# The expert's tile and the third output tile of layer 2 as seven block products, from the fourth batch on

## The reference

```
IN, HID, OUT, PART, E = (512, 2048, 512, 128, 8)
h = gelu(einsum('bni,ih->bnh', x, W1) + b1)          # x: 16 x 512 x 512
shared_x = einsum('bnh,ho->bno', h, W2) + b2         # W2: 2048 x 384
expert_x = einsum('bnh,bhp->bnp', h, We[indices]) + be[indices][:, None, :]
x = x + concatenate([shared_x, expert_x], axis=-1)
```

## Time and profile before

| | us |
|---|---|
| median of 3 runs | 1239.47 (1239.27 to 1239.71) |
| the profiled execution | 1239.46 |
| its span | 1237.6 |
| TensorE busy | 1233.2 |
| VectorE busy | 938.7 |
| ScalarE busy | 741.9 |

### The profile page before, as it was taken

One profiled execution on the slowest core, in us unless ns is written; L12 is line 12 of the kernel. 1 busy time (PEld: TensorE's weight loads), 2 busy tenths in 40 slices (PEclk: granted clock), 3 DMA queues, 4 the chain that ended last, 5 costly groups with the idle time before them and its releaser, 6 DMA issues.

```text
span 1237.6 us, 23847 instructions
## 1 busy us (share of the span) xinstructions
PE 1233.2 (100%) x9370; PEld 917.7 (74%) x9370; DVE 938.7 (76%) x1201; ACT 741.9 (60%) x944; POOL 0.2 (0%) x4
## 2 busy tenths in 40 slices
PE   9999999999999999999999999999999999999999
PEld 4456667777787777877877777778778777777775
DVE  6996677877777877768777688787787777877765
ACT  3756556666566665666566566565666656666553
POOL 0000000000000000000000000000000000000000
PEclk9999999999999999999999999999999999999999
DMA  7223123012030110202003020030300203011000
GB/s 274 100 72 125 43 77 95 1 35 69 0 102 0 55 47 0 102 0 68 33 0 102 0 98 4 0 101 0 102 0 21 80 0 102 0 50 52 1 35 35
DMA packets 25378, 64.45 MB, mean 52 GB/s; under 512 B 5120, under 2 KB 5376, under 8 KB 22144
## 3 DMA queue, kind: packets, MB, share of 16 engines
q1 hardware_dynamic: 25344, 63.99, 15.0%
HBM read 47.20 MB, written 16.78 MB: 52 GB/s over the span
## 4 chain that ended last, share of the span: by engine, by line
PE 98%; DVE 1%; issue 0%; ACT 0%; DVEq 0%
PE banks L1133 15%; PE banks L1134 15%; PE banks L1135 15%; PE out_ps L1135 9%; PE out_ps L1134 9%; PE out_ps L1133 9%; PE q_ps L1133 8%; PE q_ps L1134 8%; PE q_ps L1135 8%; DVE w_max L677 1%; PE out_ps L1346 1%; DVE x_lo L691 0%; PE banks L1145 0%; DVE w_lo L691 0%; PE q_ps L1145 0%
## 5 line engine op out<-in xcount | busy, mean ns | idle before, releaser
L1135 PE MATMUL banks<-x_hi,w_lo 128*128 128x256 f16 (+1 forms) x1704 | 467.0, 274 | 0.0
L1133 PE MATMUL banks<-x_hi,w_hi 128*128 128x256 f16 (+1 forms) x1704 | 467.0, 274 | 0.0
L1134 PE MATMUL banks<-x_lo,w_hi 128*128 128x256 f16 (+1 forms) x1704 | 467.0, 274 | 0.0
L691 DVE SCALAR_TENSOR_TENSOR h_ring<-u,scale,h_ring 128x2048 f16<-128x2048 f32 x120 | 281.1, 2343 | 6.9 <-ACT h_ring L456 4.8
L523 ACT ACTIVATE kept<-banks 128x512 f32<-128x512 f32 x180 | 106.3, 590 | 168.4 <-PE banks L1135 168.4
L1133 PEld LDWEIGHTS banks<-x_hi,w_hi 128*128 128x128 f16 x1704 | 166.7, 98 | 44.6 <-ACT kept L523 0.5
L1134 PEld LDWEIGHTS banks<-x_lo,w_hi 128*128 128x128 f16 x1704 | 166.7, 98 | 43.3 <-issue 0.3
L1135 PEld LDWEIGHTS banks<-x_hi,w_lo 128*128 128x128 f16 x1704 | 166.7, 98 | 21.8
L464 ACT ACTIVATE h_ring<-u,scale 128x2048 f16<-128x2048 f32 x56 | 112.1, 2002 | 90.7 <-DVE u L867 90.7
L554 ACT ACTIVATE u<-u,b_sb,undo 128x512 f32<-128x512 f32 x120 | 91.2, 807 | 124.1 <-DVE u L912 124.1
L899 DVE TENSOR_TENSOR u<-banks,kept 128x512 f32<-128x512 f32 x60 | 41.5, 692 | 154.4 <-PE banks L1135 144.8
(11 more groups left out here) (142 smaller groups left out, 1722.2 us busy)
## 6 DMA issues: line engine op xcount, KB each, us to landing
e_raw<-we_dram SPq DMA_DIRECT2D x16, 1024.0 KB, 4.7
out_dram<-x_raw SPq DMA_DIRECT2D x63, 256.0 KB, 2.3
x_raw<-x_dram SPq DMA_DIRECT2D x60, 256.0 KB, 3.6
h_ring<-w_dram SPq DMA_DIRECT2D x5, 1024.0 KB, 7.3
t_sum<-w2p_dram SPq DMA_DIRECT2D x2, 1024.0 KB, 4.8
w_sums<-w_dram SPq DMA_DIRECT2D x2, 768.0 KB, 14.6
x_raw<-x_dram SPq DMA_DIRECT2D x2, 512.0 KB, 5.8
h_ring<-w1f_dram SPq DMA_DIRECT2D x2, 512.0 KB, 7.2
```

The source lines that it names most:

```text
L691: return nc.vector.scalar_tensor_tensor(to, of, s, hi, ALU.mult, ALU.subtract)
L1133: nc.tensor.matmul(ps, hi, v_hi, start=start, stop=False, skip_group_check=True)
L1134: nc.tensor.matmul(ps, hi, v_lo, start=False, stop=False, skip_group_check=True)
L1135: return nc.tensor.matmul(ps, lo, v_hi, start=False, stop=stop, skip_group_check=True)
```

## The change

From batch 3 on (`FULL = 3`, "full" batches) output tiles 2 and 3 are a second pair that is taken in seven block products too (`mixed_unit`), so that layer 2 has 14 units of 6 narrow matmuls for a quarter. The pair mixes W2 and the expert's weights, so the sums of weight blocks are new for every batch: VectorE forms them (`add_es`, two halves a batch) from a second copy of W2's third tile, which SP loads again for each half together with the expert's half (`load_half`, twice two transfers of 512 KB, into `t_sum`), and both engines split them (`eh_split`, `es_split`). Four of the pair's products (P4, P5, P7, P6) share one PSUM bank by turns of two quarters; in between ScalarE copies it (`xy_keep`) and VectorE adds it (`take_xy`). The first two of the order in odd quarters are P4 and P5.

One scale serves all experts. It needs the largest magnitude of all eight: `all_e_tops_of` reads each expert's whole weights, which GpSimd loads one after another into one buffer of 1 MB, each after the reading of the one before. `e_top` and the scale for each batch are gone in full batches. `h_split` leaves out one of four blocks. 26 instead of 36 warm-up matmuls stand ahead of the first load.

```diff
-WARM = 36
+FULL = 3
+WARM = 26
+EVEN = ((0, P1, 0), (0, P2, 0), (1, P1, 0), (1, P2, 0), (0, P6, 0), (0, P5, 0), (0, P7, 0), (0, P4, 0),
+        (1, P4, 0), (1, P5, 0), (1, P3, 0), (0, P3, 0))
+ODD = ((1, P4, 0), (1, P5, 0), (0, P1, 0), (0, P2, 0), (1, P7, 1), (1, P6, 1), (1, P7, 0), (1, P6, 0),
+       (0, P6, 0), (0, P5, 0), (1, P1, 0), (1, P2, 0), (0, P7, 0), (0, P4, 0), (1, P3, 0), (0, P3, 0))
+FULL_UNITS = ((1, 2, 2, 2, 3, 1, 1), (2, 2, 2, 2, 3, 2, 3))
...
+            def load_half(b, half, par=None):
+                e = sp.value_load(idx[0:1, bass.ds(b, 1)], min_val=0, max_val=E - 1)
...
+                if half == 0:
+                    sp.wait_ge(x_lo_done, OPS * (b - 1) + P4 + 1)
+                else:
+                    sp.wait_ge(es_lo_done, 2 * half_number(b, half))
...
+            pool.wait_ge(w2_lo_done, D)
+            for e in range(E):
+                if e > 0:
+                    pool.wait_ge(all_e_max_done, e)
+                nc.gpsimd.dma_start(place(0, 1), we[e]).then_inc(all_e_loaded, 16)
...
+            def all_e_tops_of(*experts):
+                for e in experts:
+                    dve.wait_ge(all_e_loaded, 16 * e + 16)
+                    top(all_e_max[:, e:e + 1], place(0, 1)).then_inc(all_e_max_done, 1)
...
+            def add_es(b, half):
+                n = half_number(b, half)
+                a11, a12, a21, a22 = (eh_raw[:, :, k] for k in range(4))
+                dve.wait_ge(eh_loaded, 32 * n + 32)
+                nc.vector.tensor_tensor(a22, a21, a22, ALU.add).then_inc(es_added, 1)
...
+            def full_batch(b, par, loads=None):
+                sure = full(b - 1)
+                for i in (P4,) if first_full(b) else (P5, P7, P4):
+                    x_split(b, par, i)
+                c11(b, 0)
+                h_split(b - 1, 3, 1 - par)
+                x_split(b, par, P3)
+                add_ht(b - 1, 3)
+                eh_split(b, 0)
+                if not first_full(b):
+                    add_es(b, 0)
+                c22(b, 0)
+                ht_split(b - 1, 3, 1 - par)
...
+            def full_unit(b, d, unit):
+                units = ODD if d % 2 else EVEN
+                pair, i, back = units[unit]
+                if unit == (2 if d % 2 else 0):
+                    pe.wait_ge(h_lo_done, D * b + d + 1)
+                if unit == (0 if d % 2 else 4):
+                    pe.wait_ge(ht_lo_done, D * (b - PLAIN) + d + 1)
...
-            for unit in range(sum(Q_UNITS)):
+            for unit in range(len(EVEN)):
                 layer2(B - 1, D - 2, unit)
-
-            for unit in (0, 1, 6, 7, 8, 9, 2, 3, 4, 5, 10, 11, 12, 13, 14):
+            for unit in range(len(ODD)):
                 layer2(B - 1, D - 1, unit)
```

More of the change, by code:

```diff
@@ L261, in flat, with u_block, u_flat, u_tile @@
             return t[:, d, a:a + n].rearrange("p a k j c -> p (a k j c)")
+        def u_block(d, i, n):
+            return u[:, d % 2, AT[i, n]]
+        def u_flat(d):
+            return u[:, d % 2].rearrange("p a j n -> p (a j n)")
+        def u_tile(t, c):
+            i, j = c // 2, c % 2
+            a, z = AT[i, 0], AT[i, 1]
+            return t[:, a:z + 1:z - a, j]
+        def full(b):
+            return not isinstance(b, int) or b >= FULL
+        def first_full(b):
+            return isinstance(b, int) and b == FULL
+        def half_number(b, half):
+            return 2 * (b - FULL) + half
         def plain(b):
@@ L342, in reload_w2, with full_batch @@
                 sp.dma_start(w2_s_sum, w2p[half]).then_inc(w2_reloaded, 16)
-            def turn(b, par):
-                store(b, par, 0)
-                store(b, par, 1)
-                reload_x(b + 2, par, 0)
-                store(b, par, 2)
-                reload_x(b + 2, par, 1)
-                store(b, par, 3)
-                reload_x(b + 2, par, 2)
-                reload_x(b + 2, par, 3)
-                load_expert(b + 2, par, D * b + 2 * D)
+            def full_batch(b, par, last=False):
+                load_half(b, 0)
+                load_half(b, 1, None if last else 1 - par)
+                for o in range(OT):
+                    store(b - 1, 1 - par, o)
+                if not last:
+                    for o in range(OT):
+                        reload_x(b + 1, 1 - par, o)
             half = 2 * BLOCK
@@ L558, in batch @@
             def batch(b, par, last=False, sums=False, w2_s=False):
-                late = not (isinstance(b, int) and b <= 2)
                 keep(b, 0, 0)
@@ L665, in _ @@
             batch(2, 0, w2_s=True)
-            with act.Fori(0, B // 2 - 2) as pair:
-                batch(2 * pair + 3, 1)
-                batch(2 * pair + 4, 0)
-            batch(B - 1, 1, last=True)
+            full_batch(3, 1)
+            full_batch(4, 0)
+            with act.Fori(0, B // 2 - 3) as pair:
+                full_batch(2 * pair + 5, 1)
+                full_batch(2 * pair + 6, 0)
+            full_batch(B - 1, 1, True)
             h_split(B - 1, 1, 3)
@@ L1232, in product_unit @@
                             pe.wait_ge(q_taken, 3 * (b - 1 - PLAIN) + bank + 1)
-                        else:
+                        elif not full(b):
                             pe.wait_ge(out_ready[0], b)
@@ new lines, in full_unit @@
+            def full_unit(b, d, unit):
[5 more added lines that the diff above has]
+                    pe.wait_ge(ht_lo_done, D * (b - PLAIN) + d + 1)
+                done = mixed_unit(b, d - back, i) if pair else product_unit(b, d, i)
+                if unit == len(units) - 1 and d < D - 1:
+                    done.then_inc(l2_done, 1)
@@ L1255, in layer2 @@
             def layer2(b, d, unit):
+                if full(b):
+                    return full_unit(b, d, unit)
                 if plain(b):
@@ L1311, in step @@
                     layer1(b, d, i)
-                    if d == D - 1 and i == P6 and not last:
+                    if d == D - 1 and i == (P7 if full(b) else P6) and not last:
                         x_total(b + 1)
-                    for _ in range((UNITS if plain(b2) else Q_UNITS)[i]):
+                    for _ in range((UNITS if plain(b2) else FULL_UNITS[d2 % 2] if full(b2) else Q_UNITS)[i]):
                         layer2(b2, d2, unit)
                         unit += 1
-                if d == 0:
+                if d == 0 and not full(b):
                     e_total(b)
+                    if b == PLAIN:
+                        pe.wait_ge(all_e_max_done, E)
+                        total(all_e_tops, all_e_max[:, :]).then_inc(all_e_all_done, 1)
             def first_batch():
@@ L1347, in _ @@
             first_batch()
[L1348 removed]
+            for b in (1, 2, 3):
                 for d in range(D):
                     step(b, d)
[L1351 removed]
+            with pe.Fori(4, B - 1) as b:
                 for d in range(D):
```

489 lines of the change are left out of this document (434 added, 55 removed).

## The result

The changed kernel takes **1280.87 us** (median of 4 runs, 1279.31 to 1281.77), the kernel before 1239.37 in the same comparison: a ratio of 1.0333, 95% interval 1.032 to 1.0346. It is slower, as forecast, but by 41.5 us and not by 17, and outside the range.

What follows compares the result with a forecast made beforehand. TensorE, busy for the whole span, was taken to bound the kernel, so time is a count of matmuls. 1239.46 - 30.9 + 26.9 + 2.75 + 11.4 + 1.0 + 6.5 - 0.5 = 1256.6 us, range 1238 to 1268.

Steps and rivals of the forecast that it cites:

- the restart of TensorE's clock: In the reading of the experts: slow matmuls after TensorE's 12 us idle time, +2.75 us counted once, bounds 0 and three times that.
- batch 3's extra splits: Batch 3, step 0: the sums come with four extra splits, +1.0 us.
- Term 1: TensorE's columns: 168 narrow matmuls replace 96 wide ones, 2.38 us less in each of 13 batches, -30.9 us.
- Rival E: Pair's narrow matmuls in all 13 batches: dearer than they look, 0.12 us each, giving 1280.7 us; chance 0.02.
- Term 2: Reading all eight experts once, (1, 1) to (2, 1): TensorE waits on loads and readings, +26.9 us, plus 2.75 for a restart.
- Term 3: Step 0 of full batches: VectorE's c22 comes late for P3, 0.95 us in each of 12 batches, +11.4 us.
- Term 4: The end: TensorE waits 3.4 us for ht_split's low half, and VectorE's last mixing adds 3.1, together +6.5 us.
- A: Whole kernel: VectorE's new work stays inside its idle time of 17.6 us a batch, giving 1214.6 us; chance 0.08.
- C: As B, with the reading of the experts at its low end of 22 us, giving 1237.6 us; chance 0.12.
- B: Step 0 of full batches: no delay, as the load lands early or room is larger, giving 1245.2 us; chance 0.16.
- D: Step 0: the load takes 7.3 us and what follows slips 2.6 us further each batch, giving 1288 us; chance 0.05.

Runs made afterwards that it cites:

- the run with the filled stop: Changed kernel with 118 narrow matmuls on constants ahead of x_total of (1, 3), filling 12.9 of TensorE's 14.4 us wait: 1274.65 us.
- The edit: Changed kernel with ScalarE's s1_split(1) of batch 3 moved from ahead of gelus(3,2) to behind it: 1272.89 us.
- the repeat: The changed kernel run again without any edit, as a second set of runs: 1279.76 us, ratio 1.0324 to the kernel before.
- the kernel with all parts: Changed kernel with spread readings in two buffers, c22 and third keep first, s1_split(1) behind gelus, last quarter reordered, VectorE's loop written out: 1215.47 us, ratio 0.9808.
- the runs of the batch 3 edit and the tail: Changed kernel with s1_split(1) behind the gelus: 1272.89 us; changed kernel with the last odd quarter reordered and mix of bank 1 sooner: 1273.56 us.
- the kernel without the scan: Changed kernel without GpSimd's loads and the eight readings of experts, scale from W2 alone: 1249.66 us.

## Why the prediction was wrong in size

The direction and the waits on loads were right. Three steps failed: the turn of VectorE's loop was put at nothing (some 9 us), the restart of TensorE's clock was counted once (9 us), and batch 3's extra splits were priced by their work and not by their place in ScalarE's queue (3.4 us). The waits of the scan were 2.2 us longer than walked, and batch 4 was 1.3 late. (The five come to 25 us; that a short batch lost less than walked makes up for the rest.)

**Term 1, the columns: right.** 75.79 us a batch became 73.39 where nothing is late: 2.40 less, forecast 2.38. Rival E, a dearer narrow matmul, is out. The 131 ns for 512 columns of the Trainium skill (page TensorE: Matmul & The Clock Gate, section Back-to-back issue gap), which the prediction set aside, is not borne out either: by an estimate from that figure for the 96 wide matmuls and 0.109 us for the 168 narrow ones a batch would have become 5.7 us longer.

**Term 2, the scan: the waits right, the clock too small.** The trace of after has TensorE idle 3.56, 0.99, 0.54, 14.44, 5.82, 2.03 and twice a little up to (3, 0), 27.8 us in all, and with the 0.16 for each stop 29.1, for the 26.9 of the sum. The pieces fit as well (3.25, 12.35, 5.55 for the three large ones). A reading started 5.3 to 5.5 us behind the one before, not 5.0; the reload in (1, 2) and the eighth load cost less than written. (The prediction's times for the reload add up to 11.6 us and not to 12, so its 2.2 should have been 1.8; measured 1.15.) VectorE's own waits for these loads:

```profile
DVE all_e_max L911 <- DMA h_ring<-we_dram: 24.3, 5, 5.5
...
DVE h_ring L1082 <- DMA h_ring<-w_dram: 4.9, 1, 4.9
```

The other 7.5 us are time in which TensorE worked at the low clock, and for this the sum had 2.75, "once". It was not once. Of the windows of after, the three behind the other stops:

```profile
125.00:130.00 5.00, 5.00 (x27) 3.00 (x25) 3.18 (x3) 0.00 (x0) 0.00 (x0) 0.66 0.86 289
...
190.00:195.00 5.00, 4.66 (x24) 2.97 (x25) 2.45 (x2) 0.00 (x0) 0.42 (x1) 0.66 0.59 210
...
205.00:210.00 5.00, 5.00 (x28) 2.73 (x27) 2.39 (x2) 3.85 (x7) 0.00 (x0) 0.80 0.40 134
```

By the starts of the matmuls it cost 1.7, 1.5 and 1.9 us behind the stops of 3.56, 5.82 and 2.03 us, and 2.4 behind the long one. The term's own bound, "three times that" (8.25), held for the scan. The step that failed is the count: the sum allowed for one restart, in the scan, and none behind the wait of 3.4 us that it had itself put into the tail. The trace has two more outside the scan: 1.7 us behind a stop of 3.55 in batch 3, and 2.7 behind the 3.30 in the tail:

```profile
1260.00:1265.00 5.00, 5.00 (x25) 3.57 (x24) 0.75 (x1) 0.06 (x1) 0.00 (x0) 0.50 0.01 3
```

**Term 3, step 0: right in size for the short batches** (74.2 us; 0.8 us above the 73.39 of a batch without waits, where 0.95 was walked). TensorE stops there for the third `keep` first and then for `c22`, about 0.4 us each; the walk had the `keep` inside the delay by `c22`. Missing was the turn of VectorE's loop, four times 2.0 to 2.2 us of VectorE, which made the long batches 2.3 us longer than the short ones. The walk went through the instructions in program order and had no turn in it; the trace of before shows no delay by one. Whether that is because it stood in idle time there or because the shorter loop fetched nothing is open (see above). Then 1.3 us in batch 4, which took 75.58 and 75.73 us in the two profiles of the changed kernel and 74.38 in the run with the filled stop: the expert's half of SP's load landed 5.5 and 5.7 us after its issue in the first two and 4.3 in the third, and no slack is left there. I took 4.7 plus 0.2, between them.

**Batch 3: the step was wrong.** "Four extra splits: +1.0" priced the added work and not its place in ScalarE's queue. `s1_split(1)` waits for a sum that stands behind VectorE's `c12`, and the gelus that TensorE wants stand behind the split. TensorE's waits in batch 3 are 4.4 us (3.7 of them this one) where the term had 1.0, and the low clock behind them is 1.7; that is the whole of the 5.0. The edit took 5.0 us out of the batch, or 3.3 against the repeat, whose clock had not fallen.

**Term 4, the tail: the wait right, the clock left out.** 3.3 us of wait for the low half against 3.4; but the stretch from (15, 0) is +5.8 against +3.2, and the 2.7 us of low clock behind that wait make the difference.

**Rivals.** A and C fell with the scan, B with the short batches of 74.2. E's 1280.7 is the measured time within 0.2 us, and that is chance: its dearer matmuls do not exist. D's time of 1288 was nearer than the forecast too, by another mechanism: it is VectorE's turn and not the load that made batches long.

**What stays open.** The changed kernel and its variants scatter by 0.8 to 5.2 us from run to run, the kernel with all parts by 0.7. Most of what the profiles of two kernels differ by at places that no edit touches is the clock: from (4, 0) to (15, 0) it falls behind none of the stops in the changed kernel, behind two in the repeat (of 2.12 and 2.62 us, 1.65 each) and behind one, for as much, in six of the variants, while other stops of up to 2.5 us pass without it. With batch 4's load that accounts for the 3.2 us that the filled stop seemed to win in later batches, and for most of the like in the runs of the batch 3 edit and the tail. What decides whether the clock falls behind a stop is not shown, nor is what the turn of the loop cost in the kernel before.

## What to carry to other kernels

A wait is dearer than its length: here 58 us of waits brought 12 us of low clock with them. A loop turn that costs nothing now may cost 2 us once its body is longer or the idle time around it is filled, so it belongs in the walk. An addition is priced by what is queued behind it on its own engine, on every engine that it touches; an order that puts the instruction for which TensorE waits first (`c22`, the third `keep`, the gelus) won back some 16 us here without removing any work. A one-time scan of 8 MB through one buffer cost 35 us, 25 of which went with its loads, and nothing when two buffers and idle places took it.

## What the runs showed of the hardware

- VectorE's loop turn with a body of two batches: 2.0 to 2.3 us without an instruction in the changed kernel and its repeat, with one packet of instructions in each; 3.2 to 3.4 us in the kernel without the scan, with two. Written out, it is gone, and four long batches with it. The shorter loop of the kernel before has no such packets and costs nothing.
- A stop of TensorE of 14.4 us is followed by 4 us of matmuls at a granted clock of 0.50, worth 1.9 us. Behind stops of 3.5 and 2.0 us windows have 0.62 and 0.80. Up to (3, 0) the low clock added 7.5 us to 29.1 of waits, a quarter.
- The same stop of 3.55 us in batch 3 is followed by a window at 0.66 in one profile of the changed kernel and at 1.00 in the other, 1.7 us apart.
- 512 KB from SP beside another 512 KB landed 4.3, 5.5 or 5.7 us after issue, in three profiles with equal work there.
